# Normalisation and deformable 7x7 convolution: another order of the prologue's moments and filters, and of the last outputs of each unit

## The reference, cut to what matters

```python
# x: (32, 32, 56, 56) fp32, weight: (32, 32, 9), P: (2, 32, 9), bias: (32,)
kern = zeros(32, 32, 7, 7)                       # built from weight and P
for di, dj, frac in corners:                     # 4 bilinear corners
    kern = kern.at[:, cidx, ih + di, iw + dj].add(weight * frac[None])
g = x.reshape(32, 32, 1, 56, 56)                 # 32 groups of one channel
m = mean(g, (2, 3, 4)); s = var(g, (2, 3, 4))
xn = ((g - m) / sqrt(s + 1e-5)).reshape(x.shape)
out = x + conv2d(xn, kern, stride 1, padding 3) + bias
```

## Time and profile before

| | |
|---|---|
| median of 3 runs | 321.54 us (320.04 to 323.8) |
| the profiled execution | 323.41 us, of it the span of instructions 321.6 us |
| PE busy | 287.7 us (89%) |
| DVE busy | 262.0 us (81%) |
| ACT busy | 219.4 us (68%) |
| POOL busy | 174.0 us (54%) |
| mean granted clock of PE | 0.967 of full |
| DMA | 59.09 MB, mean 184 GB/s |

### The profile page before, as it was taken

How to read it: one execution, slowest core, us unless ns; L and a number is a source line. 1 busy time by engine, 2 the same in 40 slices (tenths; PEclk the granted TensorE clock), 3 DMA queues, 4 the chain that set the end, 5 groups by cost and what they waited for, 6 DMA issues and landing times.

```text
span 321.6 us, 9687 instructions
## 1 busy us (share of the span) xinstructions
PE 287.7 (89%) x3436; PEld 201.3 (63%) x3436; DVE 262.0 (81%) x358; ACT 219.4 (68%) x327; POOL 174.0 (54%) x339
## 2 busy tenths in 40 slices
PE   5920799799999999999999999999999899999990
PEld 2710466467766667677777677767777577776760
DVE  4359599989978897989797998979897989797221
ACT  2259897966968595959788786969595949471300
POOL 6242747565565839293756655565748393844000
PEclk9975699999999999999999999999999999999997
DMA  8952355979998897979797999999998949398605
GB/s 145 155 105 77 98 148 111 262 165 234 213 222 210 183 259 161 265 160 248 171 255 170 236 203 221 218 208 235 195 249 183 256 97 234 92 242 225 135 2 101
DMA packets 128255, 59.09 MB, mean 184 GB/s; under 512 B 122068, under 2 KB 122068, under 8 KB 128228
## 3 DMA queue, kind: packets, MB, share of 16 engines
q1 hardware_dynamic: 115204, 24.90, 41.6%
q0 software_dynamic: 9312, 33.04, 38.1%
q10 hardware_dynamic: 3712, 0.80, 1.3%
HBM read 12.88 MB, written 12.85 MB: 80 GB/s over the span
## 4 chain that ended last, share of the span: by engine, by line
PE 42%; DMA 10%; POOL 10%; ACT 8%; issue 7%; DVE 5%; ACTq 1%; DVEq 0%; POOLq 0%
PE ps_x L792 12%; PE ps_eo L792 11%; DMA xb<-xs 10%; PE ps_y L792 10%; PE ps_s L792 9%; POOL xn L700 5%; ACT xs L344 4%; POOL xb L669 3%; ACT junk L314 2%; DVE e L434 2%; DVE result L459 2%; POOL rtmp L675 1%; DVE xs L455 1%; ACT m L350 1%; ACT ps_y L360 0%
## 5 line engine op out<-in xcount | busy, mean ns | idle before, releaser
L669 POOL DMA_DIRECT2D xb<-xs x192 | 94.4, 498 | 61.7 <-DVE xs L455 58.8
L792 PE MATMUL ps_eo<-xs,w 128*64 128x392 f16 (+1 forms) x576 | 98.7, 324 | 0.0
L792 PE MATMUL ps_eo<-xb,w 128*64 128x392 f16 (+1 forms) x576 | 98.7, 324 | 0.0
L344 ACT ACTIVATE xs<-e 128x900 f16<-128x900 f32 x48 | 59.2, 1233 | 32.5 <-DVE e L434 31.1
L792 PE MATMUL ps_s<-xb,w 128*64 128x392 f16 (+1 forms) x384 | 69.6, 331 | 4.8 <-DMA xb<-xs 4.8
L792 PE MATMUL ps_s<-xs,w 128*64 128x392 f16 (+1 forms) x384 | 70.6, 331 | 0.5 <-ACT m L350 0.5
L792 PEld LDWEIGHTS ps_eo<-xs,w 128*64 128x64 f16 x576 | 61.6, 109 | 12.8
L792 PEld LDWEIGHTS ps_eo<-xb,w 128*64 128x64 f16 x576 | 61.6, 109 | 12.6
L792 PE MATMUL ps_x<-xs,w 128*64 128x392 f16 x384 | 67.7, 328 | 0.0
L792 PE MATMUL ps_x<-xb,w 128*64 128x392 f16 x384 | 67.7, 328 | 0.0
L455 DVE TENSOR_TENSOR xs<-e,xs 128x900 f16<-128x900 f32 x48 | 60.9, 1269 | 0.0
(11 more groups left out here) (90 smaller groups left out, 461.5 us busy)
## 6 DMA issues: line engine op xcount, KB each, us to landing
xb<-xs POOLq DMA_DIRECT2D x96, 168.8 KB, 4.2
xb<-xs POOLq DMA_DIRECT2D x96, 166.9 KB, 4.6
xraw<-x SPq DMA_DIRECT2D x124, 98.0 KB, 2.8
out<-result SPq DMA_DIRECT2D x124, 98.0 KB, 5.2
xraw<-x ACTq DMA_DIRECT2D x4, 98.0 KB, 4.1
out<-result ACTq DMA_DIRECT2D x4, 98.0 KB, 3.7
wnat<-L_conv_weight POOLq DMA_DIRECT2D x1, 36.0 KB, 3.8
pts<-L_conv_P POOLq DMA_DIRECT2D x2, 1.1 KB, 2.9
```

Source lines behind the costliest of these rows:

```text
L344: act.activation(halves(par, 0, s, count), stream(s, par, count), ACT.Copy).then_inc(hi_ready, count)
L669: pool.dma_start(dst[32 * g:32 * g + 32, 0:run - line * past], src[32 * f:32 * f + 32, line * past:run]).then_inc(shifted[par][b], DMA)
L792: last = pe.matmul(into[p:p + HALF, :, 0:PER * wide], w[:, n // 2, s, q, t, :], moving.rearrange("p n q m -> p n (q m)"), start=fresh and ...
```

## The change

It has four parts.

1. **Prologue.** PE folds the mean of unit 0 ahead of filter chunk 0 and the variance ahead of chunk 1; DVE takes the mean between the diagonals of chunks 0 and 1, and the variance ahead of the scale chain. `sums(0)` may begin when the first image has landed. The matrix `fold` is gone: PE multiplies by `eye`, and the factor goes into the two DVE instructions that read the result. The first differences come ahead of the filter sums, and `d` behind the first two low batches. The scaling of `kern` moves from DVE to ACT (`take_filters`).
2. **Units 0 and 1.** `variance(1)` leaves PE's prologue for stream 2 of unit 0; `mean(2)` moves from stream 1 to stream 6 of unit 0; `variance(2)` from stream 5 of unit 0 to stream 1 of unit 1; `mean(3)` and `variance(3)` from streams 1 and 5 to streams 3 and 7 of unit 1. Sixteen matmuls on zeros stand ahead of the first stream where two stood. ACT and DVE have a new order for both units; unit 0's batches b4 and b5 are now behind `middle(0)` on ACT.
3. **POOL.** For unit 0 all three shifts stand ahead of `normalise(1)`; before, shift 2 stood behind it.
4. **Every unit.** `outs_4(u-1)` stands behind the differences of unit u+1 in the step of unit u, where it ended step u-1. The last store waits for each image apart.

```diff
@@ sync / scalar: the last store
-            queue.wait_ge(combined, OUTS * UNITS)
             for m in range(PER):
+                queue.wait_ge(combined, OUTS * UNITS - 1 + m)
                 for g in (first, first + 2):
@@ scalar, prologue
+            take_filters(0)
+            take_filters(1)
             act.wait_ge(edges_zeroed, 2)
             high(0, 0, *BATCHES[0], first=True)
+            high(0, 0, *BATCHES[1], first=True)
             filter_high(0)
             filter_high(1)
-            high(0, 0, *BATCHES[1], first=True)
             sums(1, 1, 0)
             filter_high(2)
+            high(0, 0, *BATCHES[2], first=True)
+            high(0, 0, *BATCHES[3], first=True)
+            squares(1, 1)
+            act.wait_ge(bias_loaded, DMA)
+            middle(0, first=True)
+            high(0, 0, *BATCHES[4], first=True)
             filter_high(3)
+            high(0, 0, *BATCHES[5], first=True)
+            seed(0, 0, 0, first=True)
+            root(1)
             filter_high(4)
...
             normalise(1, 1, first=True)
...
+            for batch in BATCHES[2:]:
+                high(1, 1, *batch, first=True)
+            root(2)
+            normalise(2, 2)
@@ vector, step
                 if nxt:
                     odd_differences(u + 1, a)
                     differences(u + 1, a)
+                if not isinstance(u, int) or u:
+                    outs_4(u - 1, a)
                 if stats:
                     mean(u + 2)
...
                 outs_3(u)
-                outs_4(u, h)
@@ gpsimd
                 shift(u, u % 2, 0)
                 if u == 0:
                     shift(u, u % 2, 1)
+                    shift(u, u % 2, 2)
                 if u + 1 < UNITS:
                     normalise(u + 1)
                 if u:
                     shift(u, u % 2, 1)
-                shift(u, u % 2, 2)
+                    shift(u, u % 2, 2)
@@ tensor
+            pe.wait_ge(hi_ready, 3)
+            for n in range(8):
+                mark(n)
+            mean(1)
+            for n in range(8):
+                last = mark(n)
             last.then_inc(marked, 1)
-            mean(1)
-            variance(1)
@@ tensor, step
-                    if s == 1 and stats:
-                        mean(u + 2)
-                    if s == 5 and stats:
-                        variance(u + 2)
+                    if first:
+                        if s == 2:
+                            variance(1)
+                        if s == 6:
+                            mean(2)
+                    elif second:
+                        if s == 1:
+                            variance(2)
+                        if s == 3:
+                            mean(3)
+                        if s == 7:
+                            variance(3)
+                    elif stats:
+                        if s == 1:
+                            mean(u + 2)
+                        if s == 5:
+                            variance(u + 2)
```

More of the change, by code:

```diff
@@ L393, in filter_high @@
                 act.activation(flat(w[:, 0, dst]), flat(src), ACT.Copy).then_inc(whi_ready, 1)
+            take_filters(0)
+            take_filters(1)
             act.wait_ge(edges_zeroed, 2)
             high(0, 0, *BATCHES[0], first=True)
+            high(0, 0, *BATCHES[1], first=True)
             filter_high(0)
             filter_high(1)
[L399 removed]
             sums(1, 1, 0)
             filter_high(2)
+            high(0, 0, *BATCHES[2], first=True)
[4 more added lines that the diff above has]
+            high(0, 0, *BATCHES[4], first=True)
             filter_high(3)
+            high(0, 0, *BATCHES[5], first=True)
+            seed(0, 0, 0, first=True)
+            root(1)
             filter_high(4)
[L404 to L407 removed]
+            seed(0, 0, 1, first=True)
             sums(2, 2, 0)
             normalise(1, 1, first=True)
[L410 to L412 removed]
+            high(1, 1, *BATCHES[0], first=True)
+            high(1, 1, *BATCHES[1], first=True)
+            squares(2, 2)
+            sums(3, 3, 0)
+            for batch in BATCHES[2:]:
+                high(1, 1, *batch, first=True)
+            root(2)
+            normalise(2, 2)
+            for h in range(1, RING):
+                step(h, h, (h + 3) // RING, True, True, True)
             with act.Fori(1, UNITS // RING - 1) as it:
@@ L722, in _ @@
             for n in range(8):
-                last = pe.matmul(ps_y[:, n % 2, 0:N], zeros[:, 0:128], zeros[:, 0:N], start=True, stop=True)
-            last.then_inc(marked, 1)
+                pe.matmul(ps_y[:, n % 2, 0:N], zeros[:, 0:128], zeros[:, 0:N], start=True, stop=True)
             pe.wait_ge(weights_loaded, DMA)
@@ L731, in _ @@
             pe.wait_ge(wmax_ready, 1)
-            pe.matmul(ps_stat[0:1, 8:8 + CH], wmax[:, :], ident[:, :], start=True, stop=True).then_inc(wmax_row, 1)
+            pe.matmul(ps_y[0:1, 0, 0:CH], wmax[:, :], ident[:, :], start=True, stop=True).then_inc(wmax_row, 1)
             def fold_columns(a, b):
                 for p in (0, HALF):
-                    last = pe.matmul(ps_stat[p:p + HALF, a:b], fold[:, p:p + HALF], moments[:, a:b],
+                    last = pe.matmul(ps_stat[p:p + HALF, a:b], eye[:, p:p + HALF], moments[:, a:b],
                                      start=True, stop=True)
@@ L754, in _ @@
                 pe.wait_ge(cols_ready, k + 1)
-                if k == CHUNKS - 1:
-                    pe.wait_ge(fold_built, 1)
-                    pe.wait_ge(wmax_ready, 1)
+                if k == 0:
+                    pe.wait_ge(eye_built, 2 * GROUPS)
                     mean(0)
+                if k == 1:
+                    variance(0)
+                if k == 2:
+                    pe.wait_ge(srow_step, 7)
+                    pe.matmul(ps_s[:, 128:131], ones[:, :], srow[:, 2:5], start=True, stop=True
+                              ).then_inc(scales_in_psum, 1)
                 for n in range(4):
@@ L764, in _, with mark @@
                         last.then_inc(kern_in_psum, 1)
-            pe.wait_ge(srow_step, 7)
-            pe.matmul(ps_s[:, 128:131], ones[:, :], srow[:, 2:5], start=True, stop=True).then_inc(scales_in_psum, 1)
-            variance(0)
+            def mark(n):
+                return pe.matmul((ps_x, ps_y)[n // 2 % 2][:, n % 2, 0:N], zeros[:, 0:128], zeros[:, 0:N],
+                                 start=True, stop=True)
             pe.wait_ge(kern_ready, 2)
             pe.wait_ge(scales_ready, 1)
-            for k in range(2):
-                last = pe.matmul(ps_x[:, k, 0:N], zeros[:, 0:128], zeros[:, 0:N], start=True, stop=True)
+            pe.wait_ge(hi_ready, 3)
+            for n in range(8):
+                mark(n)
+            mean(1)
+            for n in range(8):
+                last = mark(n)
             last.then_inc(marked, 1)
-            mean(1)
-            variance(1)
             def convolve(u, par, s, nth):
@@ L796, in convolve, with step @@
                 last.then_inc(conv_done, 1)
-            def step(u, par, nth, stats, first=False):
+            def step(u, par, nth, stats, first=False, second=False):
                 for s in range(NS):
@@ L818, in _ @@
             for u in range(2):
-                step(u, u, 0, True, first=u == 0)
+                step(u, u, 0, True, first=u == 0, second=u == 1)
             with pe.Fori(1, UNITS // 2 - 2) as it:
```

112 lines of the change are left out of this document (67 added, 45 removed).

## The result

The changed kernel has a median of 331.1 us over 4 runs (329.1 to 332.24), the kernel before 321.3 us beside it: the ratio is 1.0285, with a 95% interval of 1.0243 to 1.0326. It is slower by 2.85%; the forecast was no change, and 331.1 lies outside the range. The profiled execution took 331.42 us, 8.0 more than the one of before. The top of its page shows PE busier (300.7 us against 287.7) for nearly the same instructions. The mean clock is lower there (0.942 against 0.967), but that says little: two of the four executions had 0.972 and 0.974 and took 330.77 and 329.1 us, and the record it comes from has a gap (last point of this document).

A forecast was written before the change was run, and what follows sets the result against it. PE was taken to bound the kernel from 34.6 us on. Terms +5.0 (up to unit 2's stream 3), -3.6 (every unit), -0.5 (tail) gave +0.9 on 323.41: 324.3 profiled, median 322.4, range 316.5 to 327.5.

The forecast's parts named there:

- Part 1, the prologue: Up to the first stream: root 4.7 us earlier, filters no earlier, shift 0 at 23.25, first stream at 27.3, 7.3 earlier.
- a first stream after 30: End of the prologue: listed among the signs that would show the forecast wrong; it expected 27 to 28.
- Part 2, the wait ahead of unit 1: End of unit 0: a new PE wait of 4.7 us, unit 1 starting at 48.85, 4.9 earlier than 53.75.
- Unit 1: Stream 3 at 61.5 against 61.88, after a wait of 5 us or more; slow clock charged once, at 1.45.
- Unit 2: Stream 3 in effect at 83.65 against 78.66, 5.0 us later than before, with variance(3) folded ahead of unit 1's stream 7.
- Part 3, every unit: From unit 2's stream 3 on: DVE fills its wait for last streams, shift waits nearly all go, 3.6 us less.
- Part 4, the tail: Last unit: the first image's stores start one output earlier, 0.5 us less.
- the long chain: Rival, units 2 and 3: slower from root to shift; unit 1's stream 3 at 66.2, total 327.1; chance 0.12.
- a collision of stores: Rival, every unit: later stores meet the next unit's shift 0, the 3.6 us are not won, 326.0; chance 0.13.
- The short chain: Rival, units 1 and 2: clock stays up, unit 2's shift 1 lands after 4.05, total 318.2; chance 0.25.
- The start did move: Answers the rival that the start does not move: prologue gain 5.4 us, not 7.3, total 324.3; chance 0.05.
- The rule that was weighed: POOL's xn: two-input DVE instructions contend with it; short time for unit 2, long for unit 3; no sum changes.

The follow-up runs named there:

- e9: Kernel before, with pairs of two-column fp32 matmuls added ahead of filter chunks 1 and 2, results unused: 326.09 us, ratio 1.0119.
- e3: Changed kernel with unit 3's mean folded ahead of stream 2 and its variance ahead of stream 5 of unit 1: 327.22 us, ratio 1.0159 to before.
- e4: Changed kernel with unit 2's variance folded ahead of stream 0 of unit 1, its root and normalisation moved earlier too: 324.08 us, ratio 1.0057 to before.
- e5: Changed kernel with the edits of e3 and e4 together: 322.51 us, ratio 0.9991 to the kernel before.
- e1: Kernel before, with only outs_4 moved behind the differences of unit u+1: 320.77 us, ratio 0.9977.
- e2: Changed kernel with outs_4 put back at the end of its own unit's step: 336.06 us, ratio 1.044 to the kernel before.
- e12: Kernel of e11 with e10's edit, unit 0's variance folded ahead of filter chunk 2: 320.98 us, ratio 0.997 to the kernel before.
- e10: Changed kernel with unit 0's variance folded ahead of filter chunk 2 instead of chunk 1: 330.66 us, ratio 1.0291 to the kernel before.
- e11: Kernel of e5 with units 0 and 1 reordered on ACT and DVE, b4 and b5 ahead of middle(0): 321.97 us, ratio 0.9985 to the kernel before.
- e8: Kernel before, with only unit 0's folds moved ahead of filter chunks 0 and 1, with eye, and the scales behind spread(0): 323.54 us, ratio 1.0037.
- e6: Changed kernel with 6 more matmuls on zeros ahead of the weights and 4 ahead of the first fold: 329.99 us, ratio 1.0239 to the kernel before.

## Why the prediction was wrong, point by point

In the profiled execution the forecast was 324.3 and the result 331.42, a miss of 7.1 us. The mechanism was the right one: late folds hold up the shifts ahead of stream 3 of units 1 and 2. Three terms of the sum failed. The prologue let the filter chunks keep the time of before, and they took 3.7 us longer; the slow clock behind the wait ahead of stream 3 of unit 1 was charged at 1.45 and cost 2.9, and came once more behind the wait ahead of unit 1; and of the 3.6 us to be won by the moved outputs from unit 2 on, 1.5 came. By its own steps:

- **Part 1, the prologue.** The order of events was right up to the root (squares at 9.60, root at 13.63, forecast 9.5 and 13.35). Then "the filters are no earlier" failed: by it PE starts them 0.4 later and ACT scales them at about 19.0. The chunks began 0.5 later (9.30 for 8.80) and ended 4.2 later (21.32 for 17.12), and ACT scaled the second half of the filters at 21.36. That the chunks take their 8.3 us of before was put in without a reason: the instructions that pass were counted, and not whether the half rate ends where the folds now stand. e9 shows that it doesn't. Shift 0 was issued at 26.08 instead of 23.25, and it landed 4.7 us later, where 4.05 was assumed: first stream at 30.79, 3.5 late. The forecast itself named "a first stream after 30" as a sign of error.
- **Part 2, the wait ahead of unit 1.** It was forecast at 4.7 and measured at 4.62, at the place named and by the chain named (`outs_2(0)` at 43.10, `e` 44.25, low b1 46.76, shift 48.52). With the landing again 0.65 longer, unit 1 starts 4.4 behind the forecast of 48.85, 3.5 of it from the prologue.
- **Unit 1.** The clock was charged once, at 1.45, behind the wait ahead of stream 3. It came twice, and the first time on the chain: behind the wait ahead of unit 1 stream 0 took 3.99 us at 0.50, so `spread(2)` got its fold only at 57.38 and the root (57.57) came behind that and not behind ACT's b5. The slow clock put no more than 0.7 us on the chain there, since b5 itself ended at 56.88 (forecast 52.95), late with the start of the unit. The small instructions and `xn` took 2.3 and 2.11 (forecast 2.0 and 2.17), the landing 4.7 again, 0.7 over the forecast: stream 3 at 66.93 instead of 61.5, 5.4 late, 1.0 more than the start. A second releaser stood there unforeseen: `middle(1)` is behind the normalisation of unit 2 on ACT, and stream 3 waits for it too (3.09 us, to 65.34). That normalisation held both.
- **Unit 2.** From stream 3 of unit 1 to the fold of unit 3 it took 77.59 - 66.93 = 10.7 us instead of 9.15: the cold stretch costs 2.9, not 1.45, because the clock stayed at 0.50 to about 72.7, while the earlier trace rows had shown 2.9 us of streams at the half rate in one place and I took that length for the rule. Fold to shift issue was 6.4 (forecast 6.25), the landing 4.85 (forecast 6.0), the wait ahead of stream 3 1.27 at full clock, so the further 0.75 of clock that I charged there did not come. The step "5.0 us later than before" became 10.15. Late folds were the right mechanism, in the right place, at the wrong size; e3, e4 and e5 show that without them the loss is gone.
- **Part 3, every unit.** DVE's wait for `ps_y` went from 22.0 to 3.7 us, as forecast, but this gave 1.5 us of the 3.6 claimed. A wait of 1.07 stayed ahead of stream 3 of unit 3 (107.00), which I take for an echo of the late moments, and one of 0.64 at 260. In e1, which has no wait there, the stretch gained 2.6. So the term was too large even by itself: I had turned nearly every us of waiting into time.
- **Part 4, the tail.** 0.6 for 0.5: right.

The terms of the miss, in us: prologue 3.5, the start of unit 1 another 0.9, stream 3 of unit 1 another 1.0, the clock behind it 1.5, fold to shift 0.1, landing -1.15, the clock not paid in unit 2 -0.75, every unit 2.1, tail -0.1: 7.1.

Of the rivals, the long chain had the sign that decides it (stream 3 of unit 1 after 63.8), but not its mechanism: behind the root of unit 2 neither the small instructions (2.3 for its 3.15) nor `xn` (2.11 for 3.07) nor the landing (4.7 for 6.8) was long. What was long was the way to the fold. Its price, 327.1, lacked the same two terms, chunks and clock; that it lies nearest to the result of all is luck. That the move adds a collision of stores fell by e1 and e2. The short chain had stream 3 of unit 2 at 79.5; it came at 88.81. The start did move: the first stream came 3.8 us earlier, with shift 0 issued only 2.5 earlier, so the landing of shift 0 was not what held it before. The rule that was weighed held: `xn` took 2.11 us at 60.14, with DVE idle from 59.2 to 62.36, and 3.19 at 80.82 beside DVE; the Trainium skill (SBUF — State Buffer, "Who interferes with whom") and the rows agree, and as forecast it decided nothing.

What stays open: why shift 1 of unit 1 lands 5.6, 5.5 and 6.3 us after its first issue in e4, e5 and e12 and 4.7 in the changed kernel, with no load or store issued before the last 0.8 us of that time in any of them; what sets the time at which the rate rises in the chunks (e10, e12); and how much of the 4.6 us wait ahead of unit 1 can go at all; e11 took 1.0 off it, and orders beyond that were not tried.

## What to carry to other kernels

When small steps of the next units' statistics are pushed later in a hand-written order, follow them to the transfer at the end of their chain and compare that with the time at which the main engine comes by: here folds that stood one stream (e4) and two streams (e3) too late cost 7.0 and 3.9 us, since they came late by the stall ahead of them and by the slow restart as well. Do not carry instruction durations of TensorE across a reordering without asking at which of its two rates it will run there; charge each wait of several us with a slow restart of its own, as a range and not as one length, and look whether that restart stands on the chain.

## What the runs showed of the hardware that was not expected

- **Matmuls of two columns between long ones kept TensorE at 1.2 GHz.** In the kernel before, chunks 0 and 1 stood together and the rate doubled within chunk 1 (12.34 to 13.95: four matmuls in 1.03 us instead of 1.91). With a pair of two-column fp32 matmuls between chunks 0 and 1 it did not double until the chunks were over, though PE was busy from 8.3 to 20.3 in e9. From the first chunk's start to the last one's end it took 12.0 us in the changed kernel, e8 and e9, and 8.3 before: 3.7 more for 0.4 to 0.7 us of short instructions. The ten traces with such a pair there agree (in e6 only the first few matmuls were faster); in the four without (before, e1, e10, e12) the rate rose within chunk 1, in e12 only at its end. Once it had risen, a pair did not bring it down (14.90 in the kernel before, 16.42 in e12).
- **Work ahead did not hold the clock.** In e6, with 18 matmuls on zeros, the rate was high at 9.11 and the granted clock fell to 0.50 between 9.4 and 9.8, with PE busy without a gap from 8.90 on.
- **The slow restart was longer than the one seen before, and not of one length.** Behind waits of 4.6 and 4.2 us streams ran at 0.50 from 53.2 to 59 and from 66.9 to 72.7, 5.8 us each, against 2.9 in the earlier trace rows. The length does not follow the wait: behind 4.22 us in e5 the slow matmuls ended at 58.1, after 3.4 us, behind 3.22 in e11 after 3.1 (51.5 to 54.6), and behind 3.25 in e12 after 5.7 (51.3 to 57.0). Behind waits of 1.0 to 1.3 us (e5, and 88.81 in the changed kernel) streams ran at full clock; behind about two it went either way, full at 82.64 in e4 (2.30), 0.50 at 89.95 in e2 (2.02).
- **The record of the granted clock can read 1.00 ahead of its first change.** For 8 to 14 us of the kernel before it says 1.00, while four chunk matmuls there take 1.9 us, nearly twice the 1.03 from 13.95 on; in e8 it says 1.00 through all the slow chunks. In the prologue durations are the better witness.
